# Selective scan and routed FFN on one core: five of sixteen input products moved from VectorE to GpSimd

## The chip, the cores and the metric

The kernel runs on one core of one Trainium2 chip. The metric is the device time of one execution in microseconds (us), and lower is better.

## The reference

x is (4, 1024, 1024), the context (4, 1024, 512), all float32. First comes a selective state space layer, then a routed expert layer.

```python
# layer 1: the scan. hidden = context, z = layernorm(x)
x = einsum('ed,bld->bel', in_proj_w, hidden)        # 1024 channels, 1024 times
u = silu(causal_conv4(x) + conv_b)
x_dbl = einsum('ke,bel->bkl', x_proj_w, u)          # dt_lo (32 rows), B (16), C (16)
delta = softplus(dt_proj_w @ dt_lo + dt_proj_b)
A = -exp(A_log)                                      # 1024 channels x 16 states
for t:  state = state * exp(delta_t * A) + (delta_t * u_t) * B_t
        y_t = sum over the 16 states of state * C_t
y = (y + D * u) * silu(z)
x = x + y
# layer 2: switch over a whole sequence, top 2 of 8 experts per batch entry, 16 heads of 64
gate, top_idx = top_k(softmax(layernorm(x) flattened @ switch_w.T + switch_b), 2)
o = sum over both experts of gate * (gelu(xh @ w1.T + b1) @ w2.T + b2)
x = x + ((layernorm(x) + o) @ w3.T + b3)
```

## The kernel before

The scan is cut into 64 **steps**: 4 batch entries x 2 halves of time (512 columns each) x 8 blocks of 128 channels. In the code a step is g (or st within its batch entry), the half is th, the block j. A step treats its 16 states n in 8 **slots** q of two states each (PAIRS = SLOTS = 8). The first eight steps of a batch entry are first-half steps (th = 0: their scans start from 0.0, and GpSimd keeps the last column of each h), the last eight are second-half steps (their scans start from that column).

For each state five things happen:

1. ScalarE computes dA = exp(delta * A), L1100, into a ring of RA = 4 tiles in SBUF. An activation waits until the scan four back has freed its tile.
2. VectorE multiplies delta * u with row n of B (L1299, `times_b`), into one of two PSUM banks, M0 for even and M1 for odd n (`duB`). It reads `du`, a copy in PSUM of `du_s`.
3. VectorE scans (L1326, `tensor_tensor_scan`) dA and this product into h, 128x512. h is a ring of RH = 3 pairs.
4. GpSimd multiplies the pair with C in place (L799), 128x1024.
5. TensorE sums the pair into the transposed y (`yT`) with transposing matmuls (L862, `sum_pair`).

Beside that, once in a step: GpSimd computes `du_s` = delta * u for the next step (L756, `du_of`), ScalarE copies it to PSUM (L1055, `copy_du`), and TensorE's dt projection (L854, the entry "v"), softplus on ScalarE (L1043, L1045, L1049: Abs, Exp, Ln) and its last part on VectorE (L1221, `softplus_c`, at the end of slot 3) prepare the next delta. ScalarE makes the first tap of the convolution, VectorE the three others (L1191, in slot 1 or 2). ScalarE computes u * D (L1088, `uD`, the first thing in a step) and normalises the transposed x (L1107, `xz`), which TensorE turns in slot 4. In slot 6 ScalarE does two silu's with their table loads. VectorE multiplies y with silu(z) in slot 2 (L1243), GpSimd adds x in slot 3 (L786).

The expert layer of batch entry b - 1 is fitted between the slots of batch entry b by a hand-written plan (class `Schedule`): each of its pieces has a slot, and every engine runs its queue in the order of the slots. Its pieces are the logits (L976), the routing, transposes and their evictions (L905, L1151), hidden layers (L918) with gelu (L1162, with a table load before and one after, L1059), expert outputs (L928, added by VectorE at L1277), and the output tiles (L995, added at L1285). The last entry's expert layer is the tail, after the scan. SyncE issues all DMAs, among them the rows of B and C, one load per pair and half.

The list `POOLED` is empty. The code has a path for states in it already: `pooled(n)` is true for odd n with n // 2 in the list, `times_b` of GpSimd (L759) makes their product into `duB_s`, and `VEC` lists the states whose product VectorE makes.

Of the kernel before, what the change touches and what calls it, by code (L numbers as in the profile page):

```python
# [24 lines left out]
PAIRS = N // 2  # L25
# [10 lines left out]
ALL = NB * STEPS  # L36
AHEAD = 10
UR = 10
POOLED = ()
NV = N - len(POOLED)  # L40
TAIL = 240
W3C = 4
# [9 lines left out]
def pooled(n):  # L52

    return n % 2 == 1 and n // 2 in POOLED

# [194 lines left out]
def build(nc, x, ctxT, w_inT, conv_w, conv_b, x_projT, dt_projT, dt_b, A_log, D, sw, sw_b,  # L250
# [4 lines left out]
    with ExitStack() as ctx:  # L255
# [5 lines left out]
        def sem(name, start=0):  # L261


            s = ctx.enter_context(nc.semaphore(name))
            counts.append((s, 1 + start))
            return s
# [125 lines left out]
        duB_s_done = sem("duB_s_done")  # L392
# [39 lines left out]
        def turns(slot):  # L432
            for b in range(NB + 1):
                for t in range(len(PLAN.slots[b])):
                    slot(b, t)
# [4 lines left out]
        def count(b, *name):  # L440

            return PLAN.use[(b, *name)][1]
# [5 lines left out]
        def late(b, t, q):  # L448

            return t % SLOTS == q and (t >= SLOTS or b > 0) and (b < NB or t < SLOTS)  # L450
# [8 lines left out]
        def pool_index(g, n):  # L459
            return len(POOLED) * g + sum(pooled(m) for m in range(n))  # L460

        def f_index(b, k):
            return 2 * TB * b + k

        def logit_batch(b, k):
            return b - 1 if k >= TB else b
# [247 lines left out]
        @block.gpsimd  # L714
        def _(pool):
            e = pool
            e.memset(ident[:], 0.0).then_inc(ident_step, 1)
            e.wait_ge(ident_step, 2)
            e.affine_select(out=ident[:], in_=ident[:], compare_op=ALU.not_equal, fill=1.0, base=0,
                            pattern=[[-1, P]], channel_multiplier=1).then_inc(ident_step, 1)  # L720
            e.wait_ge(masks, 1 + MASKS)

            def ln1_rstd(b):

                e.wait_ge(ln1_step, 1 + 3 * J * (b + 1))
                e.wait_ge(zn_done, 1 + STEPS * b)
                e.tensor_tensor(r1[:], mv1[:, :, 1], minus_half[:, 0:1].broadcast_to([P, J]), ALU.pow).then_inc(ln1_rs, 1)

            e.wait_ge(const_loaded, 1 + 16 * CONSTS)
            e.memset(cw9[:], 0.0).then_inc(edge_step, 1)  # L730
            e.wait_ge(edge_step, 1 + 1)
            for i in range(HL):
                e.tensor_copy(cw9[:, :, i, i:HL], cw[:, :, 0:HL - i]).then_inc(edge_step, 1)
            e.wait_ge(edge_step, 1 + 1 + HL)

            def edges(b):


                n = 3 * b + 1 + HL
                e.wait_ge(halo_done, 1 + J * (b + 1))  # L740
                e.wait_ge(col_done, 1 + J * b)
                e.tensor_tensor(edge9[:], cw9[:], halo[:].unsqueeze(2).broadcast_to([P, J, HL, HL]), ALU.mult) \
                    .then_inc(edge_step, 1)
                e.wait_ge(edge_step, 1 + n + 1)
                e.tensor_tensor(edge[:], edge9[:, :, :, 0], edge9[:, :, :, 1], ALU.add).then_inc(edge_step, 1)
                e.wait_ge(edge_step, 1 + n + 2)
                e.tensor_tensor(edge[:], edge[:], edge9[:, :, :, 2], ALU.add).then_inc(edge_step, 1)
                e.wait_ge(edge_step, 1 + n + 3)
                e.tensor_tensor(edge[:], edge[:], cb[:].unsqueeze(2).broadcast_to([P, J, HL]), ALU.add) \
                    .then_inc(edge_done, 1)  # L750

            def du_of(g, delta_ready):

                e.wait_ge(evac[S], delta_ready)
                e.wait_ge(du_done, 1 + g)
                e.tensor_tensor(du_s[:], delta[:, g % 2, :], u[:, g % UR, :], ALU.mult).then_inc(du_s_done, 1)  # L756
                e.wait_ge(du_s_done, 1 + g + 1)

            def times_b(g, q):  # L759

                n, i = 2 * q + 1, pool_index(g, 2 * q + 1)
                if g % J == 0:
                    e.wait_ge(bc_loaded[q], 1 + 32 * (g // J + 1))
                if i >= 2:
                    e.wait_ge(h_done, 1 + scan_of_pooled(i - 2) + 1)
                e.tensor_tensor(duB_s[:, i % 2, :], du_s[:], Bb[:, n, :], ALU.mult).then_inc(duB_s_done, 1)

            def scan_of_pooled(i):
                g, k = divmod(i, len(POOLED))
                return N * g + 2 * POOLED[k] + 1  # L770

            edges(0)
            ln1_rstd(0)
            du_of(0, 1 + AHEAD // 2 + 2)
            for q in (0, 1):
                if q in POOLED:
                    times_b(0, q)

            def slot(b, t):
                st, q = divmod(t, SLOTS)  # L780
                g, c = STEPS * b + st, TH * b + st // J
                if late(b, t, 3):

                    e.wait_ge(xt_loaded, 1 + 16 * g)
                    e.wait_ge(yg_done, 1 + g)
                    e.tensor_tensor(xt[:], szT[:], xt[:], ALU.add).then_inc(x1_done, 1)  # L786
                if b < NB:
                    th, j = divmod(st, J)
                    s = 2 * (q % RH)
                    e.wait_ge(h_done, 1 + N * g + 2 * q + 2)  # L790
                    if th == 0:

                        e.tensor_copy(state[:, j * N + 2 * q:j * N + 2 * q + 2], h[:, s:s + 2, T - 1]) \  # L793
                            .then_inc(saved, 1)
                    if j == 0:
                        e.wait_ge(bc_loaded[q], 1 + 32 * (c + 1))
                    if th == 0:
                        e.wait_ge(saved, 1 + PAIRS * (J * b + j) + q + 1)
                    e.tensor_tensor(h[:, s:s + 2, :], h[:, s:s + 2, :], Cb[:, 2 * q:2 * q + 2, :],  # L799
                                    ALU.mult).then_inc(prod_done, 1)  # L800
                    if q == 4 and g + 1 < ALL:
                        du_of(g + 1, 1 + count(b, "v", st) + 1)
                    ahead = divmod(PAIRS * g + q + 2, PAIRS)
                    if ahead[0] < ALL and ahead[1] in POOLED:
                        times_b(*ahead)
                    if st == STEPS - 2 and q == 4 and b + 1 < NB:
                        edges(b + 1)
                for what, *a in PLAN.slots[b][t]:
                    if what == "rstd":
                        k = a[0]  # L810
                        f = f_index(logit_batch(b, k), k)
                        e.wait_ge(mv_step, 1 + 5 * f + 5)
                        p = logit_batch(b, k) % 2
                        if logit_batch(b, k) >= 2:
                            e.wait_ge(renorm_done, 1 + TB * (logit_batch(b, k) - 1))
                        e.tensor_tensor(r2[:, p, k:k + 1], mv[:, 1:2], minus_half[:, 0:1], ALU.pow).then_inc(rs_done, 1)
                        e.wait_ge(rs_done, 1 + f + 1)
                        e.tensor_tensor(nm2[:, p, k:k + 1], mv[:, 2:3], r2[:, p, k:k + 1], ALU.mult).then_inc(nm_done, 1)
                    elif what == "ln1_rstd":
                        ln1_rstd(b + 1)  # L820
            turns(slot)
# [179 lines left out]
        def _(act):  # L1001
            e = act
# [48 lines left out]
            def copy_du(g):  # L1051

                e.wait_ge(du_s_done, 1 + g + 1)
                e.wait_ge(duB_done, 1 + NV * g)
                e.copy(du[:], du_s[:]).then_inc(du_done, 1)  # L1055
# [18 lines left out]
            def slot(b, t):  # L1074
                st, q = divmod(t, SLOTS)
                g, c = STEPS * b + st, TH * b + st // J
# [6 lines left out]
                if b < NB:  # L1083
# [7 lines left out]
                    for n in (2 * q, 2 * q + 1):  # L1091
# [3 lines left out]
                        else:  # L1095
                            i = vec_index(g, n)
                            if i >= RA:
# [1 line left out]
                            dst = dA[:, i % RA, :]  # L1099
                        e.activation(dst, delta[:, st % 2, :], ACT.Exp,  # L1100
                                     scale=Av[:, j * N + n:j * N + n + 1]).then_inc(dA_done, 1)
                    if q == 3:

                        if st == 0:
                            e.wait_ge(ln1_done, 1 + b + 1)
                        e.wait_ge(xz_loaded, 1 + 16 * (g + 1))
                        e.activation(xz[:], xz[:], ACT.Identity, scale=r1[:, j:j + 1], bias=nm1[:, j:j + 1]) \  # L1107
                            .then_inc(zn_done, 1)
                    if q == SLOTS - 1 and g + 1 < ALL:
                        copy_du(g + 1)  # L1110
                    if q == 4 and g + 1 < ALL:
                        e.wait_ge(du_s_done, 1 + g)
                        softplus_a(g + 1, (st + 1) % 2)
                        softplus_b(g + 1, (st + 1) % 2)
# [329 lines left out]
```

## Time and profile before

| | |
|---|---|
| median of 3 runs | 2656.7 us (2654.74 to 2658.29) |
| profiled execution | 2655.29 us, span 2653.5 us |
| busy: TensorE, VectorE, ScalarE, GpSimd | 1998.5, 2238.3, 1542.8, 1446.2 us |
| mean granted TensorE clock | 0.849 of full |

The busy share of an engine is a mean over parts of the run with different limits: a prologue to about 118 us, 64 steps, and from about 2410 us a tail in which no scan runs. Engines are PE (TensorE), PEld (its weight loads), DVE (VectorE), ACT (ScalarE), POOL (GpSimd). In a timeline the first number is the start, the second the duration, both in us, and the square bracket tells how long the engine had stood idle and what ended that.

### The profile page before, as it was taken

The numbers are of one execution on the slowest core, as the hardware profiler recorded it, in microseconds if no ns is written. First come the engines' busy times: TensorE is split into PE (matmuls) and PEld (weight loads), VectorE is DVE, ScalarE is ACT, GpSimd is POOL, SyncE is SP. The second block draws the span as 40 slices with busy tenths as digits, with TensorE's granted clock in tenths as the row PEclk, the third lists the DMA queues.
The fourth block names the chain that finished last, engine by engine and source line by source line (L and its number), as shares of the span: only waits on it lengthen the run. The fifth ranks groups of instructions, "written<-read, shape, count | busy, mean of one in ns | idle before, by whom it ended". The sixth has DMA issues, their size and how long they took to land.

```text
span 2653.5 us, 29890 instructions
## 1 busy us (share of the span) xinstructions
PE 1998.5 (75%) x9360; PEld 1083.4 (41%) x9360; DVE 2238.3 (84%) x2928; ACT 1542.8 (58%) x2225; POOL 1446.2 (55%) x990
## 2 busy tenths in 40 slices
PE   5365566666676898899675798899675797895899
PEld 2143334443443344344443344344443344442233
DVE  4399999999999889998999889998999999994300
ACT  2366555555666757855676746954666858852400
POOL 0177666666765556555775555555675666662000
PEclk9677777778787899899787899899787998997899
DMA  3401241445552364466461274465560274557311
GB/s 107 179 27 59 73 164 49 158 159 191 183 182 72 112 222 135 135 210 199 160 226 67 89 242 140 127 197 191 181 223 26 78 231 146 170 184 267 150 57 62
DMA packets 200050, 386.78 MB, mean 146 GB/s; under 512 B 30642, under 2 KB 96178, under 8 KB 199892
## 3 DMA queue, kind: packets, MB, share of 16 engines
q1 hardware_dynamic: 199892, 384.87, 43.3%
q8 instruction: 75, 1.23, 0.2%
q14 instruction: 83, 0.68, 0.1%
HBM read 350.73 MB, written 34.08 MB: 145 GB/s over the span
## 4 chain that ended last, share of the span: by engine, by line
PE 37%; issue 22%; DVE 22%; ACT 9%; POOL 6%; DMA 1%; SPq 1%; DVEq 0%; ACTq 0%; POOLq 0%
PE dense L995 13%; DVE h L1326 10%; PE dense L862 8%; PE dense L833 5%; POOL h L799 5%; DVE dense L1299 5%; ACT dA L1100 3%; DVE u L1191 2%; PE dense L845 2%; PE dense L991 2%; PE dense L928 2%; PE dense L976 2%; PE dense L918 1%; ACT L1059 1%; ACT hs L1162 1%
## 5 line engine op out<-in xcount | busy, mean ns | idle before, releaser
L799 POOL TENSOR_TENSOR h<-h,Cb 128x1024 f32<-128x1024 f32 x512 | 1208.0, 2359 | 473.6 <-DVE h L1326 450.0
L1100 ACT ACTIVATE dA<-delta,Av 128x512 f32<-128x512 f32 x1024 | 702.9, 717 | 514.0 <-DVE h L1326 511.9
L862 PE MATMUL dense<-ident,h 128*128 128x128 f32 x4096 | 635.1, 310 | 274.4 <-POOL h L799 272.9
L862 PEld LDWEIGHTS dense<-ident,h 128*128 128x128 f32 x4096 | 545.4, 161 | 450.0 <-POOL h L799 353.8
L1326 DVE TENSOR_TENSOR_SCAN h<-dA,state,dense 128x512 f32<-128x512 f32 x512 | 628.1, 1264 | 56.1 <-PE dense L862 33.8
L1299 DVE TENSOR_TENSOR dense<-dense,Bb 128x512 f32<-128x512 f32 x1024 | 653.3, 684 | 4.2 <-ACT dense L1055 2.1
L1326 DVE TENSOR_TENSOR_SCAN h<-dA,dense 128x512 f32<-128x512 f32 x512 | 597.6, 1204 | 24.0 <-PE dense L862 11.3
L995 PE MATMUL dense<-w3h,xT 128*128 128x512 f32 x832 | 391.6, 604 | 0.0
L833 PE MATMUL dense<-ctxs,win 128*128 128x512 f32 x512 | 273.0, 684 | 31.2 <-DMA win<-in_w_inT 25.4
L854 PE MATMUL dense<-dtaug,dtw 33*128 33x512 f32 x128 | 104.1, 906 | 209.8 <-DVE u L1191 180.5
L793 POOL COPY state<-h 128x2 f32<-128x2 f32 x256 | 48.0, 188 | 382.0 <-DVE h L1326 380.5
L995 PEld LDWEIGHTS dense<-w3h,xT 128*128 128x128 f32 x832 | 146.9, 191 | 167.1 <-issue 167.1
L833 PEld LDWEIGHTS dense<-ctxs,win 128*128 128x128 f32 x512 | 110.8, 227 | 169.0 <-issue 138.4
L1191 DVE SCALAR_TENSOR_TENSOR u<-dense,cw,u 128x511 f32<-128x511 f32 (+2 forms) x192 | 140.5, 732 | 32.2 <-ACT u L1025 16.1
L1285 DVE TENSOR_TENSOR res<-dense,res 128x512 f32<-128x512 f32 x64 | 43.8, 685 | 122.8 <-PE dense L995 122.5
L1059 ACT ACT_TABLE_LOAD x112 | 143.7, 1283 | 2.0
L1055 ACT COPY dense<-du_s 128x512 f32<-128x512 f32 x64 | 37.6, 587 | 155.3 <-DVE dense L1299 133.3
L976 PE MATMUL dense<-sww,row 128*32 128x256 f32 x1336 | 115.3, 433 | 15.5 <-ACT row L1130 14.6
L854 PEld LDWEIGHTS dense<-dtaug,dtw 33*128 33x128 f32 x128 | 25.7, 250 | 240.9 <-issue 240.9
L928 PE MATMUL dense<-hs,w2s 128*64 128x512 f32 x224 | 74.6, 731 | 38.5 <-ACT hs L1162 38.2
L786 POOL TENSOR_TENSOR xt<-szT,xt 128x512 f32<-128x512 f32 x64 | 81.8, 1278 | 3.0 <-DVE szT L1243 3.0
L1162 ACT ACT_TABLE_LOAD x49 | 62.9, 1283 | 34.4 <-PE dense L918 34.0
(136 smaller groups left out, 1842.1 us busy)
## 6 DMA issues: line engine op xcount, KB each, us to landing
sww<-in_sw SPq DMA_DIRECT2D x170, 512.0 KB, 4.4
Bb<-bc_scratch SPq DMA_DIRECT2D x64, 512.0 KB, 4.5
Cb<-bc_scratch SPq DMA_DIRECT2D x64, 512.0 KB, 5.8
w3h<-in_sw SPq DMA_DIRECT2D x56, 512.0 KB, 7.5
w3h<-in_w3T SPq DMA_DIRECT2D x52, 512.0 KB, 4.7
row<-x_scratch SPq DMA_DIRECT2D x42, 512.0 KB, 4.7
win<-in_w_inT SPq DMA_DIRECT2D x64, 256.0 KB, 4.0
row<-in_x SPq DMA_DIRECT2D x32, 512.0 KB, 4.3
```

The lines of the kernel that those rows point to most:

```text
L799: e.tensor_tensor(h[:, s:s + 2, :], h[:, s:s + 2, :], Cb[:, 2 * q:2 * q + 2, :], ALU.mult).then_inc(prod_done, 1)
L833: mm = e.matmul(dense[:, bank, :], win[:, par, k, :], ctxs[:, k, :], start=(k == 0), stop=(k == DK - 1))
L854: e.matmul(dense[:, S, :], dtw[0:DR + 1, j * P:(j + 1) * P], dtaug[:], start=True, stop=True) \
L862: mm = e.matmul(yT[:, k, :], h[:, 2 * (q % RH) + i, k * P:(k + 1) * P], ident[:], is_transpose=True, start=False, stop=(q == PAIRS - 1 and ...
L928: mm = e.matmul(dense[HD * i:HD * i + HD, bank, :], w2s[:], hs_of(b, hp)[:, i, :], start=True, stop=True)
L976: mm = e.matmul(dense[32 * n:32 * n + 32, F2, 0:32 * E], rows[:, lo:lo + 32], weights[:, :, 32 * n:32 * n + 32], start=first, stop=(k % TB ...
L995: mm = e.matmul(dense[:, bank, :], xT_of(b, uu)[:, d, k * P:(k + 1) * P], w3[:, d, :], start=False, stop=(d == J - 1))
L1059: e.preload_act_table_set("natural_log_exp_and_others")
L1100: e.activation(dst, delta[:, st % 2, :], ACT.Exp, scale=Av[:, j * N + n:j * N + n + 1]).then_inc(dA_done, 1)
L1191: i = e.scalar_tensor_tensor(out=u[:, G % UR, s:T], in0=dense[:, bank, 0:T - s], scalar=cw[:, j, k:k + 1], in1=u[:, G % UR, s:T], op0=ALU. ...
L1299: e.tensor_tensor(duB[:, n % 2, :], du[:], Bb[:, n, :], ALU.mult).then_inc(duB_done, 1)
L1326: e.tensor_tensor_scan(h[:, 2 * (q % RH) + n % 2, :], decay, inflow, state[:, j * N + n:j * N + n + 1] if th else 0.0, ALU.mult, ALU.add) \
```

## The change

In the slots 0, 1, 2, 4 and 7 the product of the odd state (n = 1, 3, 5, 9, 15) is made by GpSimd from `du_s` in SBUF into the two tiles of `duB_s`. Each is placed behind GpSimd's product with C of an earlier pair: `NEXT_POOLED` maps that pair to the pair served, where 8 and 9 are pairs 0 and 1 of the next step. For these five states ScalarE writes dA into PSUM bank M1 (L1094), and the scan reads dA from there and the product from `duB_s`. M1 has one tile: that activation waits until the scan of state n - 2 is done. The ring of four dA tiles serves the other eleven states. GpSimd's du_s for the next step moves from slot 4 to slot 5, and waits until the five products of the step are made; softplus on ScalarE moves from slot 4 to slot 3, and xz from slot 3 to slot 2.

```diff
-POOLED = ()
+POOLED = (0, 1, 2, 4, 7)
+NEXT_POOLED = {0: 2, 2: 4, 4: 7, 6: 8, 7: 9}
...
                 e.wait_ge(evac[S], delta_ready)
                 e.wait_ge(du_done, 1 + g)
+                e.wait_ge(duB_s_done, 1 + len(POOLED) * g)
                 e.tensor_tensor(du_s[:], delta[:, g % 2, :], u[:, g % UR, :], ALU.mult).then_inc(du_s_done, 1)
...
-                    if q == 4 and g + 1 < ALL:
+                    if q == 5 and g + 1 < ALL:
                         du_of(g + 1, 1 + count(b, "v", st) + 1)
-                    ahead = divmod(PAIRS * g + q + 2, PAIRS)
+                    ahead = divmod(PAIRS * g + NEXT_POOLED[q], PAIRS) if q in NEXT_POOLED else (ALL, 0)
                     if ahead[0] < ALL and ahead[1] in POOLED:
                         times_b(*ahead)
...
-                    if q == 3:
+                    if q == 2:
 
                         if st == 0:
                             e.wait_ge(ln1_done, 1 + b + 1)
...
-                    if q == 4 and g + 1 < ALL:
+                    if q == 3 and g + 1 < ALL:
                         e.wait_ge(du_s_done, 1 + g)
                         softplus_a(g + 1, (st + 1) % 2)
                         softplus_b(g + 1, (st + 1) % 2)
```

## Rows read from the trace of the kernel before

**Rows 1.** The page: busy us of the engines, and two of the slices.

```profile
PE 1998.5 (75%) x9360; PEld 1083.4 (41%) x9360; DVE 2238.3 (84%) x2928; ACT 1542.8 (58%) x2225; POOL 1446.2 (55%) x990
...
PE   5365566666676898899675798899675797895899
...
DVE  4399999999999889998999889998999999994300
```

**Rows 2.** Busy us in eight steps: stretch, length, engines, clock, DMA.

```profile
core 0: us, PE busy (x) PEld busy (x) DVE busy (x) ACT busy (x) POOL busy (x), PEclk, DMA share, GB/s
177.69:208.63 30.94, 18.72 (x84) 12.81 (x83) 30.71 (x38) 19.56 (x32) 22.75 (x19) 0.72 0.11 34
...
512.05:545.75 33.70, 22.20 (x135) 13.22 (x128) 33.28 (x43) 20.24 (x31) 22.04 (x13) 0.75 0.49 157
...
652.15:683.81 31.66, 17.41 (x73) 12.06 (x74) 31.59 (x39) 19.67 (x32) 22.22 (x18) 0.68 0.54 185
...
826.19:864.47 38.28, 28.14 (x115) 14.80 (x113) 35.35 (x48) 34.45 (x48) 23.65 (x19) 0.82 0.21 69
864.47:912.14 47.67, 35.01 (x143) 17.04 (x142) 42.37 (x58) 35.84 (x50) 25.43 (x21) 0.82 0.25 88
912.14:948.76 36.62, 31.00 (x104) 15.71 (x104) 30.48 (x41) 18.90 (x28) 19.64 (x16) 0.91 0.64 220
...
988.22:1026.92 38.70, 38.70 (x162) 21.57 (x161) 35.95 (x43) 23.47 (x36) 22.54 (x12) 1.00 0.39 128
...
1175.19:1217.85 42.66, 42.50 (x194) 20.47 (x193) 35.79 (x43) 21.34 (x32) 25.30 (x16) 1.00 0.60 202
```

**Rows 3.** Timeline of VectorE in a plain first-half step.

```profile
197.67 2.32 DVE L1326 TENSOR_TENSOR_SCAN h<-dA,dense 128x512 f32<-128x512 f32 x2
199.91 1.27 DVE L1299 TENSOR_TENSOR dense<-dense,Bb 128x512 f32<-128x512 f32 x2
201.09 2.32 DVE L1326 TENSOR_TENSOR_SCAN h<-dA,dense 128x512 f32<-128x512 f32 x2
```

**Rows 4.** Single lines' instructions: duration in ns, least/median/most, over the whole run.

```profile
L1326 DVE TENSOR_TENSOR_SCAN h<-dA,dense x512: 1187/1208/1222, 120.6 to 2144.9; 128x512 f32<-128x512 f32 x171
L1326 DVE TENSOR_TENSOR_SCAN h<-dA,state,dense x512: 1248/1268/1282, 383.9 to 2409.1; 128x512 f32<-128x512 f32 x171
...
L756 POOL TENSOR_TENSOR du_s<-delta,u x64: 1257/1274/1286, 115.9 to 2369.2; 128x512 f32<-128x512 f32 x64
...
L1055 ACT COPY dense<-du_s x64: 572/590/592, 117.2 to 2375.7; 128x512 f32<-128x512 f32 x64
...
L1100 ACT ACTIVATE dA<-delta,Av x1024: 703/722/740, 119.7 to 2402.1; 128x512 f32<-128x512 f32 x171
```

**Rows 5.** Timeline of GpSimd in the same step.

```profile
195.09 1.27 POOL L786 TENSOR_TENSOR xt<-szT,xt 128x512 f32<-128x512 f32 x1
196.30 0.19 POOL L793 COPY state<-h 128x2 f32<-128x2 f32 x1
196.57 2.35 POOL L799 TENSOR_TENSOR h<-h,Cb 128x1024 f32<-128x1024 f32 x1
```

**Rows 6.** Timeline of ScalarE, in the same step and in one with experts.

```profile
194.36 0.63 ACT L1049 ACTIVATE delta<-delta 128x512 f32<-128x512 f32 x1
...
198.91 0.72 ACT L1100 ACTIVATE dA<-delta,Av 128x512 f32<-128x512 f32 x1 [2.31 <-DVE h L1326]
...
829.36 1.28 ACT L1162 ACT_TABLE_LOAD   x1 [1.22 <-PE dense L918]
...
837.19 1.28 ACT L1162 ACT_TABLE_LOAD   x1
...
841.06 1.33 ACT L1100 ACTIVATE dA<-delta,Av 128x512 f32<-128x512 f32 x2
```

**Rows 7.** The table of waits: in total, times, longest us.

```profile
ACT dA L1100 <- DVE h L1326: 511.9, 412, 12.7
...
DVE h L1326 <- ACT dA L1100: 31.4, 13, 6.5
```

## The prediction

> **What bounds the kernel now.** I read the page's busy shares and slices first, then cut the trace into the 64 steps of the scan (one step is eight slots, from one uD activation to the next) and asked for each engine's busy time in every step, then the timelines of one plain step and of one step with expert work, and last the table of waits. The page alone says VectorE, 84% [rows 1], but its slices show the other engines rising over a part of the run, so the share of the whole can't price this change. The steps can. The ones shown last from 31 to 48 us, and who fills them differs [rows 2]. In batch 0 and the first steps of a batch VectorE is busy for 30.71 of 30.94 us, or 33.28 of 33.70 (in every column for a step, busy against length). In the middle of a batch TensorE takes the whole of a step (38.70 of 38.70 us at a granted clock of 1.00; 42.50 of 42.66). Where the expert layers run, ScalarE is busy for 34.45 of 38.28 us and VectorE for 35.35. GpSimd is nowhere near: 21 to 26 us a step.
>
> **The change part by part.**
>
> *Five products leave VectorE.* A pair of products occupies it for 1.18 us (from 199.91 to the scan at 201.09) [rows 3], so one is worth 0.59 us. Each of the five slots of the list loses one of its two: 5 x 0.59 = 2.95 us a step, 64 x 2.95 = 189 us if VectorE bounded everything.
>
> *They arrive on GpSimd.* The nearest row is du_s, the same form (128x512 f32, both inputs and output in SBUF): 1274 ns [rows 4]; behind the product with C such an operation takes 1.21 us of the queue (195.09 to 196.30) [rows 5]. Five are 6.05 us a step. A first-half step, with its state copies, now has 22.75 us of GpSimd work, and 0.08 us is lost at each of eight copies [rows 5]: 22.75 + 6.05 + 0.6 = 29.4 us. VectorE would need 30.71 - 2.95 = 27.8 there, so GpSimd takes over as the bound of such steps. In a second-half step GpSimd has 22.04 + 6.05 = 28.1 against VectorE's 33.28 - 2.95 = 30.3, and VectorE stays the bound. Both orders are tight, so I checked the deliveries in a plain step, counted from its first scan: the product for pair 0 of the next step is made behind the product with C of pair 6, that is 0.27 + 2.35 + 1.2 = 3.8 us after scan 13 [rows 5], and needed after a product, two scans, a product and a scan, 0.6 + 2.25 + 0.6 + 1.1 = 4.6 us later. Only 0.8 us to spare: with GpSimd a slot behind, scan 1 waits for it. That is what being bound by GpSimd will look like. The others have 2 us or more.
>
> *dA of the five states goes to the one PSUM bank M1.* An activation into PSUM stands in no row with a scale vector; dA to SBUF takes 722 ns and a plain copy to PSUM 590 [rows 4]. I take 0.72 us, with 0.59 as the other bound. It lies beside the scans unless it comes late. The bank is single, so this dA may start only after the scan two states back. Such a hand-over takes little: the first scan of the pair at 197.67 [rows 3], 1.21 us long, ends at 198.88, and the dA that waited for it starts at 198.91 [rows 6]. Between that scan and the one that needs the value VectorE does a product and a scan, 0.59 + 1.13 = 1.7 us; the activation is there after 0.8. About 0.9 us to spare in a plain step: no cost. But ScalarE's lead, four values today (it waits 511.9 us in all for scans to free its ring [rows 7]), shrinks to one or two, and what ScalarE has queued between two such values is then covered less. In plain steps these are one or two activations of 0.6 to 0.8 us, inside the 2.3 us that are free between two such values (1.7 and a scan, less 0.8). Where an expert's gelu stands there, with its two table loads, the block is 837.19 to 841.06, 3.9 us [rows 6], and four of them fall into each of 12 steps.
>
> *Softplus from slot 4 to 3, xz from 3 to 2, du_s from 4 to 5.* Left behind dA 9, which must now wait for scan 7, softplus (three activations like the 0.63 us one at 194.36 [rows 6]) would end 0.7 + 1.9 = 2.6 us after scan 7, where VectorE's half of it stands: moving it is what keeps this at zero. In slot 3 it starts about when the dt product arrives, some 2 us after the last tap, and ends 2 to 3 us before VectorE asks. xz is read by TensorE in slot 4 and is early either way. du_s is needed only by the copy to PSUM in slot 7; one slot later leaves it over 1 us. It also waits for the five products of the step, the last of which stands ahead of it in GpSimd's own queue: zero. SyncE's reloads of B wait for GpSimd's products too, but these come before the product with C for which the reload waits already. All zero, unless GpSimd lags by more than two slots; then each is part of the first rival.
>
> *Scans with other operands.* A pooled scan reads dA from PSUM and the inflow from SBUF, the reverse of now. No row has that form. With or without a state from SBUF, and whatever GpSimd does beside them (it is busy for two thirds of a step), the scans stay within 1187 to 1222 and 1248 to 1282 ns [rows 4]: zero, with bounds of -0.02 and +0.06 us for each (the step from the one form to the other).
>
> The Trainium skill bears on this (SBUF — State Buffer, "Who interferes with whom"): it says that VectorE and GpSimd share a port pair, and that an operation of VectorE with two inputs in SBUF is shut out while GpSimd reads. By it a pooled scan with dA left in SBUF would collide; with dA in PSUM it has one SBUF input besides its state column and would not. The trace agrees so far as it can, by the narrow spread just named.
>
> **The sum, by kind of step.** (T is the step's length.)
> - GpSimd bounds: 3 plain first-half steps of batch 0, 30.9 - 29.4 = 1.5 each; steps 1 and 3 of batches 1 to 3 (31.66 and the like [rows 2]), 2.0 each: 4.5 + 12 = 16.5.
> - VectorE bounds and stays: 11 steps of batch 0 and steps 2, 4, 5 and 13 of the three others (4 x 3), 23 in all. I take 2.7 of the 2.95, since a part of the idle gaps will open again: 62.
> - ScalarE bounds: 12 steps with expert work (6, 7, 11, 12). In the row it has 34.45 busy of 38.28; the five values that may not run ahead push every gelu some 2 us back against the scans, and at the step's end VectorE waits for the expert's output anyway. 0.5 each, between -3 (worked in the rival) and +2.9: 6.
> - TensorE bounds: 12 steps (9, 10, 14, 15): 0.3 each, since 38.70 is 38.70: 4.
> - The step in which x_proj ends and the one behind it: 2 in batch 0, and 8 and 16 of the others, 8 in all. A chain through szT, x_proj, the split and dA sets these (T 36.62 with no engine over 31.0 busy); only its start moves up, by the products ahead of it: 1.2 each: 10.
>
> Together 98.5 us. The profiled execution took 2655.29 us (span 2653.5), 1.4 under the median of 2656.7: 2656.7 - 98.5 = 2558 us. Prologue and the tail behind 2410 us are untouched.
>
> **Rivals.**
> 1. *The leads go, and little is left.* For: ScalarE is busy nearly throughout in the expert steps, and in them a gelu between two M1 values starves VectorE, by 2.2 us ahead of the taps of slot 1 (the block ends 4.1 us after the first value, the first tap another 0.9 later, and VectorE is there at 2.8), 1 to 1.5 behind slot 2, 0.7 behind slot 4, 1.5 behind slot 6: about 6 a step, less 2.95: 12 x -3 = -36 in place of +6. With GpSimd's lag passing into TensorE's sums and on (2.0 for 2.7 in 23 steps, 1.0 in place of 1.5 to 2.0 in nine, nothing in the last two kinds), 46 + 9 - 36 = 19 us: 2638. Against: ScalarE waits for TensorE ahead of those gelus already (1.22 us [rows 6]), so a part costs nothing. 0.14 for a gain between 5 and 45.
> 2. *VectorE's whole saving arrives*, 189 us or near it, if shorter steps raise TensorE's granted clock (0.72 in a plain step, 1.00 in the full ones [rows 2]) and the lags even out. Against: TensorE's full steps run at 1.00 already, and GpSimd's 29.4 stands. A gain over 150: 2487. 0.08.
> 3. *The other side: the pooled scan is shut out by GpSimd.* If the state column counts as a second SBUF input when the inflow is in SBUF too, each of 320 scans waits for the rest of a GpSimd operation: half of 2.36 us, times the share that GpSimd is busy (29/33): 1.04 us, 332 in all: 2558 + 332 = 2890. It decides from 98/320 = 0.31 us a scan. Against: the second-half scans read dA and state from SBUF beside GpSimd today without a trace of it [rows 4]. 0.05.
> 4. *No change*, all given back at TensorE and ScalarE: 0.03.
>
> **How the numbers follow.** Mine (a gain of 45 to 150 us) 0.70. The low end is the best of every kind: 18 + 68 + 30 + 10 + 24 = 150: 2505. The high end takes in part of the first rival: 2625. Outside lie rival 2, the far part of 1, 3 and 4: 2 in 10. A measurement of this kernel can tell about 0.2% (5 us) from no change. Faster by more: 0.70 + 0.14 + 0.08 = 0.92; I take 0.91, same 0.03, slower 0.06.
>
> **What would show it.** VectorE's products down from 1024 to 704, its busy time by some 190 us; GpSimd's up by 320 x 1.27 = 407 us, to about 1850. Plain first-half steps near 29.4 with scan 1 or 5 waiting for duB_s of GpSimd; second-half steps of batch 0 near 30.5; the TensorE steps unchanged; expert steps within 1 us of now, with VectorE's waits for dA up from the present 31 us [rows 7]. Pooled scans at 1.2 to 1.27 us. I am wrong if those are longer, if GpSimd's product takes over 1.3 us, if the expert steps lengthen by 3 us, or if the steps of TensorE shorten.

## The result

The changed kernel takes 2629.12 us (median of 4 runs, 2626.54 to 2635.0) against 2656.07 us in the same sessions: a ratio of 0.9901, interval 0.9881 to 0.9920. That is 27 us faster, where 98 were forecast, and 4 us above the top of the range. The profiled execution took 2627.18 us, span 2625.4. Its page, busy us of the engines and the slices of VectorE, against [rows 1]:

```profile
PE 2004.1 (76%) x9360; PEld 1101.2 (42%) x9360; DVE 2069.5 (79%) x2608; ACT 1529.5 (58%) x2225; POOL 1829.2 (70%) x1310
...
DVE  4399999998998888797999888887998788893300
```

VectorE's busy time fell by 168.8 us (2238.3 - 2069.5) and GpSimd's rose by 383.0. Of the 169 us that VectorE no longer works, 28 left the span (2653.5 to 2625.4); the rest turned into waiting. The same eight steps show where, against [rows 2] (stretch, length, busy us of TensorE, its weight loads, VectorE, ScalarE, GpSimd, the granted clock, DMA):

```profile
core 0: us, PE busy (x) PEld busy (x) DVE busy (x) ACT busy (x) POOL busy (x), PEclk, DMA share, GB/s
...
174.42:205.47 31.05, 20.49 (x83) 14.64 (x83) 28.12 (x33) 19.42 (x31) 28.66 (x24) 0.67 0.11 34
...
495.85:527.87 32.02, 23.12 (x156) 14.06 (x155) 30.57 (x38) 19.84 (x30) 28.10 (x18) 0.89 0.61 195
...
628.07:658.48 30.41, 18.10 (x72) 12.57 (x73) 29.43 (x34) 19.41 (x31) 27.59 (x23) 0.66 0.56 198
...
796.72:837.30 40.58, 30.20 (x130) 15.16 (x128) 34.20 (x45) 34.48 (x48) 31.50 (x25) 0.87 0.24 79
837.30:880.54 43.24, 31.14 (x128) 15.56 (x126) 37.75 (x51) 35.69 (x49) 32.08 (x26) 0.84 0.24 85
880.54:915.97 35.43, 30.41 (x105) 15.70 (x106) 28.26 (x36) 18.62 (x29) 23.04 (x21) 0.95 0.68 223
...
952.62:992.76 40.14, 40.14 (x165) 22.30 (x164) 33.22 (x37) 23.52 (x37) 31.12 (x18) 1.00 0.40 126
...
1144.32:1188.16 43.84, 43.81 (x197) 21.13 (x196) 32.61 (x37) 21.10 (x32) 34.61 (x23) 1.00 0.60 206
```

The first is the plain first-half step. GpSimd's work is 28.66 us and VectorE's 28.12, and yet it lasts 31.05 us, no less than the 30.94 of before: no engine fills it. The fourth, with expert work, grew from 38.28 to 40.58. VectorE's rows of the table of waits (in total, times, longest us) name what it now waits for. First the two of the kernel before, then four of the changed one, against [rows 7]:

```profile
DVE h L1326 <- PE dense L862: 45.1, 32, 4.4
DVE xT L1277 <- PE dense L928: 32.1, 20, 6.0
```

```profile
DVE res L1287 <- PE dense L997: 132.8, 29, 7.4
DVE h L1328 <- PE dense L864: 127.3, 102, 6.2
DVE xT L1279 <- PE dense L930: 59.2, 38, 6.0
DVE h L1328 <- ACT dA L1102: 47.4, 25, 9.1
```

The line numbers are two higher in the changed kernel: L864 is L862 of before. A scan that waits for it waits for TensorE's sum of an earlier pair, which frees a tile of h. The largest row, L997 (the expert layer's output tiles), was 122.5 us before and is no news.

The waits for the sums stand at three places of a step only. The table has us in total and times, by the state of the scan that waits; "for GpSimd" is the part in which TensorE itself had stood idle for GpSimd's product with C just before the sum.

| scan of state | pairs back | before | changed kernel | for GpSimd | GpSimd's products cut short (below) | for GpSimd |
|---|---|---|---|---|---|---|
| n = 0, slot 0 | 2 | 33.5, 19 | 76.5, 36 | 14.2 | 74.5, 34 | 7.7 |
| n = 2, slot 1 | 2 | 4.3, 5 | 22.2, 28 | 11.9 | 10.8, 14 | 1.1 |
| n = 6, slot 3 | 3 | 7.3, 8 | 28.5, 38 | 0 | 28.4, 37 | 0 |

So of the 127.3 us only 26.1 have GpSimd as the last that is late. In the other 101.2 TensorE comes to the sum straight from other work of its own queue.

By kind of step, 47.5 of the 127.3 us stand in the steps that the prediction gave to GpSimd and VectorE, where before it was 6.3. Another 52.2 stand in the steps that TensorE fills, where it was 26.7: there the wait only takes the place of work that was not the limit.

The durations of the new forms are no part of it (ns, least/median/most), against [rows 4]:

```profile
L1328 DVE TENSOR_TENSOR_SCAN h<-dense,duB_s x160: 1195/1198/1217, 120.5 to 2112.6; 128x512 f32<-128x512 f32 x160
L1328 DVE TENSOR_TENSOR_SCAN h<-dense,state,duB_s x160: 1255/1259/1279, 375.8 to 2381.4; 128x512 f32<-128x512 f32 x160
...
L768 POOL TENSOR_TENSOR duB_s<-du_s,Bb x320: 1252/1272/1302, 116.0 to 2371.9; 128x512 f32<-128x512 f32 x160
...
L1102 ACT ACTIVATE dense<-delta,Av x320: 667/692/700, 119.2 to 2376.6; 128x512 f32<-128x512 f32 x160
```

And this is the wait, in the timelines of VectorE, then TensorE, then GpSimd, at the start of the plain step above:

```profile
177.84 1.22 DVE L1328 TENSOR_TENSOR_SCAN h<-dA,dense 128x512 f32<-128x512 f32 x1 [1.29 <-PE dense L864]
...
182.50 1.22 DVE L1328 TENSOR_TENSOR_SCAN h<-dA,dense 128x512 f32<-128x512 f32 x1 [1.08 <-PE dense L864]
...
176.62 1.09 PE L864 MATMUL dense<-ident,h 128*128 128x128 f32 x8 [0.49 <-POOL h L801]
180.40 1.97 PE L864 MATMUL dense<-ident,h 128*128 128x128 f32 x8 [2.69 <-POOL h L801]
186.27 2.04 PE L856 MATMUL dense<-dtaug,dtw 33*128 33x512 f32 x2 [3.91 <-DVE u L1193]
...
172.59 1.27 POOL L758 TENSOR_TENSOR du_s<-delta,u 128x512 f32<-128x512 f32 x1
173.93 0.19 POOL L795 COPY state<-h 128x2 f32<-128x2 f32 x1
174.19 2.37 POOL L801 TENSOR_TENSOR h<-h,Cb 128x1024 f32<-128x1024 f32 x1
176.53 1.26 POOL L768 TENSOR_TENSOR duB_s<-du_s,Bb 128x512 f32<-128x512 f32 x1
...
178.00 2.34 POOL L801 TENSOR_TENSOR h<-h,Cb 128x1024 f32<-128x1024 f32 x1
...
185.55 0.18 POOL L795 COPY state<-h 128x2 f32<-128x2 f32 x1 [0.21 <-DVE h L1328]
...
189.63 0.18 POOL L795 COPY state<-h 128x2 f32<-128x2 f32 x1 [1.45 <-DVE h L1328]
```

Read it as a ring. A pair of scans may overwrite a pair of tiles of h only when the pair that lies there is summed. The ring has three pairs, and because it restarts at each step, only two across the step's edge: pair 0 takes the tiles of pair 6 of the step before, pair 1 those of pair 7.

- The scan at 177.84 is the first of slot 0. It waits 1.29 us for the sum of pair 6 (176.62 to 177.71), and that for GpSimd's product with C at 174.19. Scan 13, which completes pair 6, had ended at 173.00, but GpSimd was with `du_s` until 173.86: that is the operation that the change moved from slot 4 to slot 5. It held the product with C up by 0.86 us. TensorE, busy with the sum of pair 5 until 176.13, could have used 0.49 of them, so by this estimate up to 0.49 of the 1.29 us come from `du_s`.
- The scan at 182.50 is the first of slot 1. It waits 1.08 us for the sum of pair 7 (180.40 to 182.37). Pair 7 was complete by 175.96, but its product with C stands at 178.00, behind that of pair 6 and a product with B. Then TensorE takes 1.97 us for the sum, at a granted clock of 0.50, where the one at 176.62 took 1.09 at 1.00.

Then the three taps of slot 1 keep VectorE from making new pairs, and GpSimd, the engine with the most work, stands idle for 0.21 and 1.45 us. Each engine has free time, and none can use it.

I sorted 63 steps (the last has no uD behind it) into the kinds of the prediction and took the differences of their lengths in the two traces, each from one uD activation to the next. A positive number is time won. The second column is the forecast, without the 64th step. The last column belongs to an experiment below.

| kind, steps | forecast us | changed kernel | the same with four pairs of h |
|---|---|---|---|
| GpSimd bounds, 9 | 16.5 | -3.4 | 9.5 |
| VectorE bounds, 23 | 62 | 31.7 | 61.0 |
| ScalarE bounds (experts), 12 | 6 | -9.4 | -0.4 |
| TensorE bounds, 12 | 4 | -2.1 | -3.5 |
| x_proj and behind, 7 | 9 | 9.3 | 11.4 |
| all | 97 | 26.2 | 78.0 |

These are single executions, one of each kernel.

### The profile page after: what moved, and what is told of

The parts are those of the page before. It is cut to its first block, busy times and chain, and to the rows that moved or that the text cites. A ratio compares the mean times of both kernels' runs of the same rounds, so it can differ in the third digit from the quotient of the medians.

```text
span 2625.4 us, 29612 instructions
## 1 busy us (share of the span) xinstructions
PE 2004.1 (76%) x9360; PEld 1101.2 (42%) x9360; DVE 2069.5 (79%) x2608; ACT 1529.5 (58%) x2225; POOL 1829.2 (70%) x1310
## 4 chain that ended last, share of the span: by engine, by line
PE 42%; issue 17%; POOL 14%; DVE 14%; ACT 10%; DMA 1%; SPq 1%; DVEq 0%; POOLq 0%; ACTq 0%
PE dense L997 16%; PE dense L864 10%; POOL h L801 10%; DVE h L1328 6%; PE dense L835 4%; PE dense L993 2%; DVE u L1193 2%; PE dense L930 2%; POOL duB_s L768 2%; ACT L1164 2%; PE dense L847 2%; DVE dense L1301 2%; ACT hs L1164 2%; PE dense L978 2%; PE dense L856 2%
## 5 line engine op out<-in xcount | busy, mean ns | idle before, releaser
L864 PE MATMUL dense<-ident,h 128*128 128x128 f32 x4096 | 657.7, 318 | 249.4 <-POOL h L801 249.1
L864 PEld LDWEIGHTS dense<-ident,h 128*128 128x128 f32 x4096 | 568.1, 166 | 425.2 <-POOL h L801 317.1
L1102 ACT ACTIVATE dense<-delta,Av 128x512 f32<-128x512 f32 x320 | 220.8, 690 | 588.0 <-DVE h L1328 587.2
L1328 DVE TENSOR_TENSOR_SCAN h<-dA,state,dense 128x512 f32<-128x512 f32 x352 | 439.2, 1271 | 106.4 <-PE dense L864 73.6
L1102 ACT ACTIVATE dA<-delta,Av 128x512 f32<-128x512 f32 x704 | 481.3, 712 | 50.8 <-DVE h L1328 48.6
L1328 DVE TENSOR_TENSOR_SCAN h<-dA,dense 128x512 f32<-128x512 f32 x352 | 417.9, 1210 | 73.3 <-PE dense L864 53.7
L1301 DVE TENSOR_TENSOR dense<-dense,Bb 128x512 f32<-128x512 f32 x704 | 462.6, 682 | 4.2 <-ACT dense L1057 2.1
L768 POOL TENSOR_TENSOR duB_s<-du_s,Bb 128x512 f32<-128x512 f32 x320 | 407.0, 1272 | 0.1
L997 PE MATMUL dense<-w3h,xT 128*128 128x512 f32 x832 | 391.7, 604 | 0.0
L835 PE MATMUL dense<-ctxs,win 128*128 128x512 f32 x512 | 262.3, 661 | 37.4 <-DMA win<-in_w_inT 28.5
L997 PEld LDWEIGHTS dense<-w3h,xT 128*128 128x128 f32 x832 | 147.0, 191 | 167.2 <-issue 167.2
L1328 DVE TENSOR_TENSOR_SCAN h<-dense,state,duB_s 128x512 f32<-128x512 f32 x160 | 201.8, 1261 | 0.0
L1328 DVE TENSOR_TENSOR_SCAN h<-dense,duB_s 128x512 f32<-128x512 f32 x160 | 192.1, 1201 | 0.0
```

The source lines that it names most:

```text
L835: mm = e.matmul(dense[:, bank, :], win[:, par, k, :], ctxs[:, k, :], start=(k == 0), stop=(k == DK - 1))
L864: mm = e.matmul(yT[:, k, :], h[:, 2 * (q % RH) + i, k * P:(k + 1) * P], ident[:], is_transpose=True, start=False, stop=(q == PAIRS - 1 and ...
L997: mm = e.matmul(dense[:, bank, :], xT_of(b, uu)[:, d, k * P:(k + 1) * P], w3[:, d, :], start=False, stop=(d == J - 1))
L1102: e.activation(dst, delta[:, st % 2, :], ACT.Exp, scale=Av[:, j * N + n:j * N + n + 1]).then_inc(dA_done, 1)
L1301: e.tensor_tensor(duB[:, n % 2, :], du[:], Bb[:, n, :], ALU.mult).then_inc(duB_done, 1)
L1328: e.tensor_tensor_scan(h[:, 2 * (q % RH) + n % 2, :], decay, inflow, state[:, j * N + n:j * N + n + 1] if th else 0.0, ALU.mult, ALU.add) \
```

## The experiments

The first set had two theories: **Q**, that GpSimd's own time is what costs, and **M**, that the one bank M1, which takes ScalarE's lead, does.

### GpSimd's products cut short

```diff
-e.tensor_tensor(duB_s[:, i % 2, :], du_s[:], Bb[:, n, :], ALU.mult)
+e.tensor_tensor(duB_s[:, i % 2, 0:64], du_s[:, 0:64], Bb[:, n, 0:64], ALU.mult)
```

> GpSimd's five products cover 64 of their 512 columns (the other columns of duB_s stay zero, so the scans of these states get a wrong inflow); every instruction, wait and place in a queue stays. Theory Q (GpSimd's queue: its time delays the products with C, these delay TensorE's sums, and with three pairs of h VectorE waits for the sums) expects most of the missing gain back, 2550 to 2580 us, with VectorE's waits for the sums from 127 us down to the 45 us of the kernel before. Theory M (the one bank M1 takes away ScalarE's lead) expects it to stay at 2610 to 2629 us, with the steps with expert work unchanged.

Measured: 2616.31 us, ratio to before 0.9865 (0.9841 to 0.9890). That is 13 us under the changed kernel. VectorE's waits for the sums are 113.7 us still. Theory Q is refuted as the main cause: the time of GpSimd's five products costs 13 us here. The time lies in theory M's range, which alone doesn't show M. The table of places above tells why it gives so little: the waits for which GpSimd is last fall from 26.1 to 8.8 us, and the larger part, where TensorE's own queue is last, stays. In the plain step the second wait is gone; the first is 1.36 us still, with TensorE going from the input projection straight into the sums of pairs 5 and 6.

### dA of the five states in SBUF

```diff
 if pooled(n):
-    e.wait_ge(h_done, 1 + max(N * g + n - 1, 0))
-    dst = dense[:, M1, :]
-else:
-    i = vec_index(g, n)
-    ...
+i = N * g + n
+if i >= RA:
+    e.wait_ge(h_done, 1 + i - RA + 1)
+dst = dA[:, i % RA, :]
```

The scans read dA of all states from this ring.

> The five dA go into the ring of four tiles in SBUF, as all sixteen did before, with GpSimd's products at full size. Theory M expects 2560 to 2600 us. Theory Q expects 2620 to 2635 us. If VectorE's scans with two inputs in SBUF are shut out while GpSimd reads, as the port rule says, the pooled scans take clearly longer than 1.26 us and the kernel is slower than before, 2700 to 2900 us.

Measured: 2692.57 us, 1.0158 (1.0130 to 1.0186), slower than before. The pooled scans, in durations (ns, least/median/most) of that kernel's lines, and GpSimd's products:

```profile
L1324 DVE TENSOR_TENSOR_SCAN h<-dA,duB_s x160: 1192/1820/3371, 121.9 to 2172.1; 128x512 f32<-128x512 f32 x160
L1324 DVE TENSOR_TENSOR_SCAN h<-dA,state,duB_s x160: 1252/1514/3044, 399.0 to 2444.8; 128x512 f32<-128x512 f32 x160
...
L768 POOL TENSOR_TENSOR duB_s<-du_s,Bb x320: 1256/1283/2309, 117.4 to 2435.5; 128x512 f32<-128x512 f32 x160
```

With both inputs in SBUF a scan takes up to 3371 ns, 2.2 us above its least, near the length of one product with C (2.36 us). In the changed kernel, with dA in PSUM, the same scans stay within 1195 to 1217 and 1255 to 1279 ns. The Trainium skill (SBUF — State Buffer, "Who interferes with whom") says that a VectorE instruction with two SBUF inputs contends with a GpSimd instruction that reads SBUF, and that one with at most one, outside the modes that use both ports, does not. Both measurements agree with it. So dA in PSUM is what makes the change pay. On M and Q the run says nothing, since the port costs more than either.

### Both

The two edits above together.

> Both at once: products of 64 columns (wrong inflow in the rest) and dA of all states in the SBUF ring. Both theories expect the most that the change could give with TensorE's full steps as they are: 2500 to 2550 us. Less 'short products alone' gives what M1 costs, if the scans stay at 1.2 to 1.27 us.

Measured: 2601.84 us, 0.9801 (0.9777 to 0.9826). Both theories fall: with GpSimd's time and M1 taken away, 53 of 189 us arrive. A part of the shortfall is the port, for the scans still meet the products with C (VectorE is busy for 31.0 us in the mean of batch 0's 16 steps, against 29.6 in the run with short products alone), but VectorE still waits 80.4 us for the sums.

### The moves alone

```diff
-POOLED = (0, 1, 2, 4, 7)
+POOLED = ()
```

> The list is empty again, only the moves stay (softplus in slot 3, xz in slot 2, du_s in slot 5). Both theories: no change against before, 2645 to 2665 us. If softplus in slot 3 stands waiting for TensorE's dt product in front of dA 8, it is slower, 2670 us or more.

Measured: 2650.97 us, 0.9991 (0.9976 to 1.0006; 2640.94 to 2657.10). No change, as expected. So with three pairs of h the five products are worth 2651.0 - 2629.1 = 22 us (24 by the two ratios to before).

The waits for the sums, which stayed at 113.7 and 80.4 us in the runs with short products, gave theory **H**: the ring of h. To fit a fourth pair, 4 KB a partition are taken from the switch weights' rings; a control has the smaller rings alone.

### The control for the fourth pair

```diff
-RING_A, RING_B, RING_T = 8, 3, 19
+RING_A, RING_B, RING_T = 7, 2, 18
```

> The control for the next kernel: the changed kernel with the ring of switch weight tiles cut from three tiles to two (8 to 7 and 19 to 18 for the other two rings), which frees 4 KB a partition. Every theory: 2625 to 2650 us, as the logits alone get less lead.

Measured: 2632.88 us, 0.9931 (0.9908 to 0.9954).

### Four pairs of h

```diff
-RH = 3
+RH = 4
...
-e.wait_ge(prod_summed, 1 + PAIRS + PAIRS * g + (q - RH + 1 if q >= RH else min(q - 1, 0)))
+e.wait_ge(prod_summed, 1 + PAIRS + PAIRS * g + q - RH + 1)
```

> The same with a ring of four pairs of h in place of three; at the step's edge, where the ring of three restarts and is only two deep, it stays four deep. Theory H (VectorE, with fewer products between its scans, now runs into TensorE's sums through the ring of h; 127 us of waits against 45) expects 30 to 60 us under its control and VectorE's waits for the sums under 30 us. Theory Q (GpSimd's time) expects at most 13 us, what the short products gave. Theory M expects no change.

Measured: 2581.10 us, 0.9739 (0.9708 to 0.9770): 52 us under its control, and the fastest kernel of the study that computes the whole. Theory Q's 13 us and theory M's nothing fall. Waits of scans for sums are gone from the table, and those for dA fell from 47.4 to 18.5 us; 34.0 us in 7 waits are left to which the profile gives no releaser; the kernel before with four pairs has 28.3 of them in 8. The windows of the plain first-half step and of a plain second-half step, and the timeline of VectorE in the first:

```profile
174.82:204.06 29.24, 19.07 (x81) 13.46 (x80) 27.97 (x33) 19.31 (x32) 28.54 (x24) 0.71 0.12 36
...
484.75:515.53 30.78, 22.76 (x147) 13.34 (x146) 30.57 (x38) 19.73 (x31) 28.05 (x18) 0.83 0.60 187
```

```profile
178.21 1.22 DVE L1328 TENSOR_TENSOR_SCAN h<-dense,duB_s 128x512 f32<-128x512 f32 x1 [0.75 <-POOL duB_s L768]
```

29.24 us with GpSimd busy for 28.54 and a scan waiting for duB_s is what the prediction had for the changed kernel (29.4), and 30.78 its 30.5. The table above shows it by kind: with the fourth pair the steps of VectorE give 61.0 of a forecast 62. The edit makes the ring deeper and, as eight pairs divide by four, ends the restart at the edge. No run tells the two apart; by the places of the waits, 98.7 of the 127.3 us stood at the edge (n = 0 and 2).

The scan that waits 0.75 us is scan 1. Its product stands behind pair 6's product with C, and that again behind `du_s`.

### Four pairs of h in the kernel before

The same edit; `duB_s`, unused there, is cut to one column to make room.

> The kernel before with four pairs of h (duB_s, which it never uses, gives its place). Theory H: little, 0 to 20 us faster, since VectorE waited for the sums for 45 us only, in large part where TensorE itself is full. If it gains as much as the changed kernel does from the fourth pair, the ring is no part of why the change gave little.

Measured: 2628.24 us, 0.9917 (0.9887 to 0.9948), 25 us faster on medians, a little more than H expected. It comes from other places: of 30 us in its profiled steps the 12 expert ones give 15.6, TensorE's 7.0, VectorE's 7.3 and GpSimd's -0.6, where in the changed kernel the fourth pair gives 61.0 - 31.7 + 9.5 + 3.4 = 42 us in the kinds of VectorE and GpSimd.

### Three states in place of five

```diff
-POOLED = (0, 1, 2, 4, 7)
+POOLED = (2, 4, 7)
```

> The changed kernel with three states (n = 5, 9, 15) given to GpSimd in place of five. By VectorE's time alone it saves 0.59 x 3 x 64 = 113 us in place of 189, so if VectorE were the bound it is slower than five, 2600 to 2610 by proportion of nothing lost. Theories H and M: the two products left out (n = 1, 3) stand where VectorE waits for the sums and where M1 follows on itself, so it is no slower than five: 2615 to 2635 us.

Measured: 2643.57 us, 0.9970 (0.9952 to 0.9989). Here my expectation was wrong: it is 14 us slower than five. Three products are worth 7 us, the two for n = 1 and 3 another 14. They are no dead weight, though they stand where VectorE waits. By kind, the profiled steps of three win 2.3 us over those of five in GpSimd's steps, as expected, and lose 5.8 in VectorE's, 4.6 in the expert ones and 4.4 in TensorE's. Why these lose was not shown.

### Four pairs of h and no products moved

The fourth pair, the smaller rings, and the empty list.

> Four pairs of h, the shorter weight rings and the moves, with the list empty: what the five products are worth with the fourth pair is this kernel less the changed one with four pairs (2581). Theory H: 2625 to 2640 us, so 45 to 60 us for the products, where the ring of three gave 22 (2651 with the moves alone, 2629 with all).

Measured: 2627.80 us, 0.9893 (0.9874 to 0.9911). So with four pairs the five products are worth 2627.8 - 2581.1 = 47 us, where three pairs gave 22. By the ratios to before it is 41 against 24: the difference is 17 to 25 us.

### Four pairs of h and short products

> The changed kernel with four pairs of h and the shorter weight rings, and GpSimd's five products cut to 64 of 512 columns (wrong inflow in the rest). With the ring out of the way GpSimd's own time should come up as the next limit in the plain first-half steps: 9 to 30 us under 2581. If it gives under 5 us, GpSimd's time limits nothing at all.

Measured: 2560.15 us, 0.9641 (0.9625 to 0.9657): the time of GpSimd's products now costs 21 us. The same plain step as above:

```profile
173.65:201.72 28.07, 18.82 (x84) 13.29 (x83) 27.93 (x33) 19.38 (x32) 24.02 (x24) 0.76 0.13 37
```

VectorE is busy for 27.93 of 28.07 us. The step is 2.87 us shorter than the 30.94 of before: nearly all of the prediction's 2.95, once neither the ring nor GpSimd stands in the way.

### M1's wait alone

```diff
 i = vec_index(g, n)
+if n in (1, 3, 5, 9, 15):
+    e.wait_ge(h_done, 1 + max(N * g + n - 1, 0))
```

> The moves with the list empty, as before, and one thing of the five states kept: ScalarE may start dA of n = 1, 3, 5, 9, 15 only when the scan of n - 2 is done, as it must for bank M1. Nothing else of the change. Against the moves alone (2651 us): theory M expects 15 to 30 us more, nearly all in the 12 steps with expert work and in those behind them; theory H expects 0 to 5.

Measured: 2683.56 us, 1.0107 (1.0089 to 1.0124), against 2650.97 with the moves alone: M1's wait by itself costs 33 us, somewhat more than theory M expected. The 0 to 5 of theory H fall: the ring of h is not the only cause. ScalarE's wait for scans in that kernel and in the one with the moves alone:

```profile
ACT dA L1104 <- DVE h L1330: 684.1, 364, 11.5
```

```profile
ACT dA L1102 <- DVE h L1328: 378.9, 331, 12.7
```

(Before, it was 511.9 us.) Against before, the steps of the profiled execution lose 30 us: 17.3 in the twelve expert steps, 8.2 in TensorE's, 5.3 and 2.1 in GpSimd's and VectorE's, and x_proj's win 2.7. Not "nearly all" in the expert steps, but the greater part. How the late dA gets there shows in the changed kernel's second-half expert step, in the timelines of ScalarE, TensorE and VectorE:

```profile
2233.44 0.69 ACT L1102 ACTIVATE dense<-delta,Av 128x512 f32<-128x512 f32 x1 [2.45 <-DVE h L1328]
...
2246.46 1.97 PE L930 MATMUL dense<-hs,w2s 128*64 128x512 f32 x4 [4.33 <-ACT hs L1164]
...
2248.47 0.75 DVE L1279 SCALAR_TENSOR_TENSOR xT<-dense,b2s,xT 128x512 f32<-128x512 f32 x1 [2.94 <-PE dense L930]
```

ScalarE stands 2.45 us for the scan that frees M1 and is busy from there to the end of the step; it reaches the step's last gelu (2245.09) late, TensorE stands 4.33 us for it, and VectorE 2.94 us for the expert's output. The step (2212.01 to 2250.55) lasts 38.54 us; before it lasted 35.49.

### Four states with four pairs

`POOLED = (0, 2, 4, 7)`, with the fourth pair and the smaller rings.

> The changed kernel with four pairs of h, the shorter weight rings, and four states given to GpSimd (n = 1, 5, 9, 15, in every other slot) in place of five. It gives back 0.59 x 64 = 38 us of VectorE's time, against at most a fifth of what M1 costs (33 us) and of GpSimd's time (21 us), 11 us. Theory H with its parts as measured: somewhat slower than 2581, 2585 to 2605 us. If the three M1 values in a row (n = 1, 3, 5) were the harm, it is as fast or faster.

Measured: 2591.37 us, 0.9762 (0.9746 to 0.9778), 10 us slower than five. Each product is worth about 9 to 10 us there (36 for four, 47 for five), and three M1 values in a row are no special harm: taking the middle one away did not help.

## Why the prediction was wrong

- *Durations and counts.* Right: 1272 ns for GpSimd's product (1274 forecast), 692 for dA to PSUM (0.72), the pooled scans within 1195 to 1279 ns, and 0.59 us a product on VectorE, shown nearly whole by the run with four pairs and short products. The products' group on VectorE fell by 190.7 us (653.3 to 462.6), its whole busy time by 169: that is counted without the overlaps of neighbours, and fewer products have fewer of them. The scans' busy time, all forms together, is unchanged (1225.7 and 1228.7 us). GpSimd's new group is the 407.0 us forecast.
- *GpSimd as the bound of the plain first-half steps, 29.4 us.* **This is the step that failed**, with the next. The working checked only that GpSimd's products with B arrive in time. It did not check the way back: product with C, TensorE's sum, and the tile of h that the scan three pairs on (two across the step's edge) overwrites. The profile before had the row, 45.1 us of scans waiting for L862; the prediction mentions these sums only inside a rival, and never compared the ring's depth with the slots that VectorE was about to shorten. Even the check that was made left out `du_s`, which the change itself puts ahead of pair 6's product with C: with its 1.21 us the 3.8 becomes 5.0, and only 4.6 were free. The move of `du_s`, put at zero, may cost up to 0.49 us of this step's first wait, and by the same estimate at most 6 of the 76.5 us at n = 0 over the run. No run put `du_s` elsewhere. The step stayed at 31.05 us. With four pairs it is 29.24.
- *VectorE's 23 steps, 2.7 us each.* 31.7 us instead of 62, by the same ring: their waits for the sums rose from 5.6 to 29.6 us, and with four pairs they give 61.0. In 20.5 of the 29.6 us TensorE's own queue was last, and not GpSimd, which the prediction took for the danger.
- *ScalarE's 12 steps, +0.5 each.* -9.4 us instead of 6. The prediction saw that ScalarE's lead shrinks and put most of the cost at zero; M1's wait alone costs 33 us over the run. Waits for an M1 value itself are only 0.8 us: the cost comes through late gelus.
- *TensorE's 12 steps, +0.3.* -2.1 instead of 4. TensorE has a granted clock of 1.00 in them before and after and is busy nearly throughout (38.70 of 38.70 us, then 40.14 of 40.14 in the same step).
- *The moves at zero.* Right with the list empty: 2650.97 against 2655.24 us, within the noise. Beside the products the move of `du_s` is open, as said above.
- *x_proj's steps, 1.2 each.* Right: 9.3 us in seven.
- *Rivals.* The first, that the leads go, given 0.14 and 2638 us, came nearest in its time: 2629 was measured. Its two ways are there in part. That the number is so near is in part luck: it put the expert steps at -36 us (they lost 9.4), and the steps of VectorE and GpSimd at 55 won (they won 28). The whole saving (0.08) did not come, nor a scan shut out by GpSimd (0.05); the second is real with dA in SBUF, and dA in PSUM averts it. Its price was too high by its own condition: only the 160 second-half scans have a state column, so 1.04 us each is 166 us and not 332.
- *The range.* It ends at 2625, a gain of 32 us, while the chances count gains of 45 to 150 for it. And the time free between two M1 values is 1.7 + 1.2 - 0.8 = 2.1 us, not 2.3. Neither changes the account.

The budget of the 189 us: 22 arrived. The ring of three holds back another 25 (47 - 22 by the medians, 17 by the ratios), and GpSimd's time 21 once the ring is wider; these three, 68 us, were measured together, as 2627.8 - 2560.2. M1 was measured only by itself, with three pairs and no products moved: 33. With it the sum is 101, an estimate. The other 88 us would lie in the steps that TensorE fills, in the expert steps and in x_proj's chain, where VectorE's time was not the limit before. That is argued from the steps, not tried.

## What to carry to other kernels

When work moves off the busiest engine, walk every ring around the whole loop, not only the forward deliveries. The engine that becomes faster between two waits can need a deeper ring, and a ring that restarts at a loop's edge is shallower there than its size. The engine named by a late delivery need not be the one to relieve: here most of the late sums waited in TensorE's own queue, and a deeper ring gave 52 us where shorter work on GpSimd gave 13. An engine given more work can hurt without being full: at 28.7 busy us of 31.05, GpSimd was too late at one slot and idle two slots on. And a buffer of one, put into the queue of an engine that serves several others, is priced by what stands behind it: here 33 us for five waits a step, most of it in the steps with expert work.

## What the runs showed of the hardware

- A scan with two inputs in SBUF, beside GpSimd's products, took 1820 and 1514 ns in the median and up to 3371 (without and with a state column), against 1198 and 1259 with dA in PSUM; GpSimd's own product rose from 1272 to 1673 ns in the mean. The state column in SBUF does not count as an input in this: the changed kernel's scans with it stay within 1255 to 1279 ns.
- TensorE's sum of a pair (8 matmuls) took 1.09 us at 176.62, behind 0.49 us of idle time and at a granted clock of 1.00, the upper of its two levels (2.4 GHz). At 180.40, behind 2.69 us of idle time, it took 1.97 us at 0.50, the lower one (1.2 GHz). In the run with short products it took 1.09 us behind 1.30 us of idle time. So in this step TensorE is slowest at returning h just where it has been idle longest.
